# Expert feed-forward: who rounds the gated values, and in which order VectorE prepares the parts

## The reference, cut to what matters

```python
logits = x @ gate_w + gate_b
top_w, top_idx = jax.lax.top_k(softmax(logits), 2)      # 8 experts, 2 per token
h   = jax.nn.silu(x @ w1[e]) * (x @ w3[e])              # 256 -> 1024, for the chosen experts e
out = sum over the two experts of weight * (h @ w2[e])  # 1024 -> 256
x   = x + tanh(g_ffn[1]) * out
```

## Time and profile before

| | |
|---|---|
| median of 3 runs | 2627.19 us (2626.43 to 2630.02) |
| the profiled execution's own time | 2611.73 us |
| its span | 2610.0 us |
| TensorE matmul busy | 2107.1 us, 81% of the span |
| VectorE busy | 1935.4 us, 74% |
| ScalarE, GpSimd busy | 1022.2 us and 1016.1 us, 39% each |
| the 39 blocks | from about 1775 us to the end of the span |

### The profile page before, as it was taken

The page is one execution under the profiler, slowest core; times in us unless marked ns, Lnnn a source line. Parts: engine busy times, 40 slices in busy tenths (PEclk is TensorE's granted clock), DMA queues, the critical chain, the costliest instruction groups (busy, mean ns, idle before and its releaser), DMA issues. The chain is left out here.

```text
span 2610.0 us, 40439 instructions
## 1 busy us (share of the span) xinstructions
PE 2107.1 (81%) x13358; PEld 1479.3 (57%) x13358; DVE 1935.4 (74%) x3725; ACT 1022.2 (39%) x1581; POOL 1016.1 (39%) x554
## 2 busy tenths in 40 slices
PE   5898899747788888898888898406888888888887
PEld 3566666633234343434343435306888888888887
DVE  7999999837686867686768743605888888888886
ACT  2343344322355453545444453203444444444443
POOL 7988888622112030302021101273444444443343
PEclk9899999876799999999999998558999999999999
DMA  7000000021001010101010001233555555555552
GB/s 283 10 9 9 11 9 9 1 61 30 23 19 33 9 41 2 41 3 39 12 31 21 1 1 65 90 129 130 190 181 175 191 181 182 178 180 181 180 176 83
DMA packets 124788, 208.89 MB, mean 80 GB/s; under 512 B 9981, under 2 KB 88430, under 8 KB 124660
## 3 DMA queue, kind: packets, MB, share of 16 engines
q1 hardware_dynamic: 114024, 181.97, 20.9%
q0 software_dynamic: 10624, 25.26, 2.7%
q10 hardware_dynamic: 12, 0.01, 0.0%
HBM read 177.58 MB, written 33.18 MB: 81 GB/s over the span
## 5 line engine op out<-in xcount | busy, mean ns | idle before, releaser
L1218 DVE CUSTOM_DVE_ANT_0 x_dump<-x_ps,x_bias_q 128x512 bf16<-128x512 f32 x512 | 343.0, 690 | 66.5 <-PE x_ps L906 47.9
L1072 ACT ACTIVATE x_PT<-x_ps 128x1024 f32<-128x1024 f32 x256 | 255.0, 1021 | 311.0 <-PE x_ps L916 311.0
L843 POOL TENSOR_TENSOR x_rs<-x_ve,x_half 128x3 f32<-128x3 f32 x32 | 28.0, 876 | 719.6 <-DVE x_ve L1151 719.6
L1742 ACT ACTIVATE e_silu<-m_ps 128x256 f32<-128x256 f32 x312 | 118.8, 381 | 479.2 <-PE m_ps L1683 479.2
L906 PE MATMUL x_ps<-x_KS,x_QS 96*128 96x512 bf16 x512 | 207.5, 413 | 36.5 <-DVE x_mx L1218 33.4
L1781 DVE TENSOR_TENSOR e_gated<-e_silu,m_ps 128x256 f32<-128x256 f32 x312 | 122.4, 419 | 124.3 <-ACT e_silu L1742 115.3
L915 PE MATMUL x_ps<-x_bias_k,x_ident_b 128*128 128x512 bf16 x512 | 198.7, 388 | 19.2 <-issue 10.2
L1784 DVE CAST e_g_hi<-e_gated 128x512 fp32r<-128x512 f32 x156 | 209.4, 1343 | 5.3
L1683 PE MATMUL m_ps<-e_x_lo,m_hi 128*128 128x256 f32 x640 | 182.8, 286 | 26.0 <-issue 24.3
L1683 PE MATMUL m_ps<-e_x_lo,e_hi 128*128 128x256 f32 x608 | 180.3, 296 | 25.7 <-issue 25.7
L916 PE MATMUL x_ps<-x_QS,x_KS 99*128 99x512 bf16 x512 | 198.4, 388 | 0.0
(11 more groups left out here) (275 smaller groups left out, 6043.2 us busy)
## 6 DMA issues: line engine op xcount, KB each, us to landing
m_raw<-in_L_ffn_w_dram SPq DMA_DIRECT2D x117, 1024.0 KB, 5.2
expert_in<-a_blank SPq DMA_DIRECT2D x1, 10062.0 KB, 28.4
e_x<-expert_in SPq DMA_DIRECT2D x39, 258.0 KB, 8.1
x_mask_q<-in_mask_dram SPq DMA_DIRECT2D x32, 256.0 KB, 2.7
x_mask_k<-in_maskT_dram SPq DMA_DIRECT2D x32, 256.0 KB, 2.9
a_cT<-in_ctxT_dram SPq DMA_DIRECT2D x32, 128.0 KB, 2.2
x_cT<-in_ctxT_dram SPq DMA_DIRECT2D x32, 128.0 KB, 2.1
out_dram<-X SPq DMA_DIRECT2D x1, 4096.0 KB, 13.6
```

What stands on the lines that cost most here:

```text
L1072: act.activation(PT[u % 2][:, 2 * pr:2 * pr + 2, :], ps_st[pr], ACT.Exp).then_inc(exp_done[pr], 1)
L1218: dve.tensor_tensor_reduce(out=dump[i % 2][:, :], in0=bank, in1=bias_q[:, q, :], scale=1.0, scalar=NEG, op0=ALU.add, op1=ALU.max, accum_ou ...
L1742: act.activation(silu[f % 2][:, :], ps_h[f % 4][:, 0:BLK], ACT.Silu).then_inc(silu_done, 1)
```

## The change

The rounding `g_hi` leaves VectorE: ScalarE makes it, one pair at a time, in `gated_high`, after the silu of the following pair's first chunk. `gated` gets a second buffer, and VectorE makes the products of pair k before the difference of pair k - 1. The low part of the next block's matrix 1 moves from behind the gate into it, behind the difference of pair 1.

```diff
-            gated = sb("gated", [P, 2, BLK])
+            gated = two("gated", [P, 2, BLK])
...
+                def gated_high(j, k):
+                    act.wait_ge(gated_done, FC * j + 2 * k + 2)
+                    act.activation(g_hi[:, 2 * k:2 * k + 2, :], gated[k % 2][:, :, :], ACT.Copy).then_inc(g_high, 1)
...
                         act.activation(silu[f % 2][:, :], ps_h[f % 4][:, 0:BLK], ACT.Silu).then_inc(silu_done, 1)
+                        if f in (2, 4, 6):
+                            gated_high(j, f // 2 - 1)
                         if f in (1, 3, 5) and following:
                             high_part(act, j + 1, 1 - p, f // 2)
+                    gated_high(j, FC // 2 - 1)
...
-                    if not (isinstance(j, int) and j == 0):
-                        low_part(dve, j, p, 1)
...
+                    for k in range(FC // 2):
+                        if k > 1 or not (isinstance(j, int) and j == 0):
+                            dve.wait_ge(g_parts, FC // 2 * j + k - 1)
+                        for n in range(2):
+                            f = 2 * k + n
+                            dve.wait_ge(silu_done, FC * j + f + 1)
+                            dve.tensor_tensor(gated[k % 2][:, n, :], silu[n][:, :], ps_h[f % 4][:, BLK:2 * BLK], ALU.mult)\
                                 .then_inc(gated_done, 1)
-                        dve.wait_ge(gated_done, n + 1)
-                        steps.done(dve.tensor_copy(g_hi[:, f:f + 2, :], gated[:, :, :]))
-                        steps.wait()
-                        dve.tensor_tensor(g_lo[:, f:f + 2, :], gated[:, :, :], g_hi[:, f:f + 2, :].bitcast(F32), ALU.subtract)\
-                            .then_inc(g_parts, 1)
-                        if f == 0 and following:
-                            low_part(dve, j + 1, 1 - p, 0)
-                        dve.wait_ge(g_parts, FC // 2 * j + f // 2 + 1)
+                        if k:
+                            remainder(j, k - 1)
+                        if k in (0, 2) and following:
+                            low_part(dve, j + 1, 1 - p, k // 2)
+                    remainder(j, FC // 2 - 1)
+
+                def remainder(j, k):
+                    dve.wait_ge(g_high, FC // 2 * j + k + 1)
+                    dve.tensor_tensor(g_lo[:, 2 * k:2 * k + 2, :], gated[k % 2][:, :, :], g_hi[:, 2 * k:2 * k + 2, :].bitcast(F32), ALU.subtract)\
+                        .then_inc(g_parts, 1)
```

More of the change, by code:

```diff
@@ L1603, in experts @@
             silu_done, gated_done, g_parts = sem_("silu_done"), sem_("gated_done"), sem_("g_parts")
-            chain, y_left, y_out = sem_("chain"), sem_("y_left"), sem_("y_out")
+            g_high, y_left, y_out = sem_("g_high"), sem_("y_left"), sem_("y_out")
             labelled, blanks, before_in = sem_("labelled"), sem_("blanks"), sem_("before_in")
@@ L1759, in _ @@
             def _(dve):
-                steps = Steps(dve, chain)
                 def x_low(j, p):
@@ L1770, in x_low @@
                     dve.tensor_copy(label[p][:, :, :].bitcast(I32), xb[p][:, :, D:WIDE].bitcast(I32)).then_inc(labelled, 1)
-                    if not (isinstance(j, int) and j == 0):
-                        low_part(dve, j, p, 1)
                 def gate(j, i, p, following=True):
[L1776 to L1781, removed]
-                                .then_inc(gated_done, 1)
-                        dve.wait_ge(gated_done, n + 1)
-                        steps.done(dve.tensor_copy(g_hi[:, f:f + 2, :], gated[:, :, :]))
-                        steps.wait()
-                        dve.tensor_tensor(g_lo[:, f:f + 2, :], gated[:, :, :], g_hi[:, f:f + 2, :].bitcast(F32), ALU.subtract)\
-                            .then_inc(g_parts, 1)
-                        if f == 0 and following:
-                            low_part(dve, j + 1, 1 - p, 0)
-                        dve.wait_ge(g_parts, FC // 2 * j + f // 2 + 1)
+                    for k in range(FC // 2):
[5 more added lines that the diff above has]
+                            dve.tensor_tensor(gated[k % 2][:, n, :], silu[n][:, :], ps_h[f % 4][:, BLK:2 * BLK], ALU.mult)\
+                                .then_inc(gated_done, 1)
+                        if k:
[7 more added lines that the diff above has]
+                        .then_inc(g_parts, 1)
                 def add_y(j, p):
```

## The result

The changed kernel takes 2592.22 us (median of 4 runs, 2585.09 to 2597.55) against 2626.81 us of the kernel before beside it: ratio 0.9871, 95% interval 0.9836 to 0.9906. It is faster by 1.3%; 17 us slower had been forecast, and the time lies under the stated range. The profiled execution took 2588.63 us, its span is 2586.9 us. The expert blocks take 811 us of it (from TensorE's first transpose at 1775.87), before 835 us (from 1775.06): 24 us less in the profiled executions.

What follows compares the result with a forecast made beforehand. TensorE's two waits a block, 1.41 and 1.35 us, with VectorE and GpSimd excluding each other, were taken as the bound. Block -5, old falls -17, new falls +39 gave +17 us: 2628.7 profiled, 2644 by the median; range 2600 to 2675.

Steps and rivals of the forecast that it cites:

- The collision: Near the block's end, GpSimd's low part of matrix 2 locks out VectorE's difference of pair 2; TensorE waits 2.8 us.
- the "issue" wait: TensorE's wait at the block's end for VectorE's low part of matrix 1, 1.35 us a block, forecast to go.
- ScalarE's rounding: Rounding of 128x512 on ScalarE, taken as 0.60 us from the row of the same size, costing almost nothing.
- The landing of the scatter: Wait from scatter to gather on GpSimd, taken as about 2 us instead of 5.82 with loads spread out.
- The block: Next block starts at 2287.95 instead of 2288.09: -0.14 us, times 38 blocks -5 us.
- The clock: TensorE's clock falls from 2.4 to 1.2 GHz after the new 2.8 us wait in 26 of 38 blocks: +39 us.
- The falls of before: Eight stretches at TensorE's lower clock in the kernel before, taken to cost 17 us and to go.
- The price of 1.5 us a fall: Time a block loses when TensorE's clock falls after one idle piece, taken as 1.5 us.
- 8 in 13: Of 13 TensorE idle pieces of 1.74 us or more before, 8 were followed by a clock fall.
- The second rival: Same VectorE-GpSimd collision, but TensorE's clock holds as one lucky alignment repeats; 2605 to 2620 us, chance 0.16.
- the difference of 5.49 us: VectorE difference begun at 1854.47, 5.49 us instead of 0.69, cited as evidence that GpSimd's low part locks differences out.
- The rival of GpSimd getting in behind both differences: GpSimd enters after both last differences, TensorE becomes the bound; block some 17.8 us, 2494 us in all, chance 0.14.

Runs made afterwards that it cites:

- run with matrix 1 alone: Kernel before, with only the low part of the next matrix 1 moved inside the gate and the rounding left on VectorE; 2718.29 us, ratio 1.0384.
- the first experiment: Changed kernel, with GpSimd's low part of matrix 2 held back until the next labels are copied; 2478.63 us, ratio 0.9477.
- run with ScalarE's rounding alone: Changed kernel, with the low part of matrix 1 put back behind the gate, after the label copy; 2613.26 us, ratio 0.9989.

## Why the prediction was wrong, by its steps

- The collision: right. The place (difference of pair 2, behind the low part of matrix 1), the size of the wait (2.8 us worked out, 2.7 measured), its being one piece before the third pair, and the end of the "issue" wait came as written.
- ScalarE's rounding: 0.62 us against 0.60 taken. VectorE's low part of matrix 1 came 10.31 us into the block (2120.57, its first silu being at 2112.05, 1.79 us in), worked out as 10.35.
- The landing of the scatter: 2.23 us against 2 taken, before 5.82.
- The block: 20.47 us against 20.70. Two pairs of `project` behind the wait took 2.85 us, not 3.00, and GpSimd was done 0.09 us earlier. So -0.37 us a block, -14 us, where the sum had -5.
- The clock, the term that was mis-sized: the sum had 26 falls, +39 us. Measured are 2 from 1800 us on, some 3 us, and none in the last 36 blocks. The price of 1.5 us a fall was right, the number of falls was not.
- The falls of before: taken off at 17 us. In the trace of before the 22 blocks that meet no stretch at the lower clock are 20.83 us apart in the mean, like the reference block, and all 38 are 21.18, so they cost 13 us.
- Added up for the profiled executions: -14 for the block, -13 for the falls of before, +3 for the two left, -24 us, which is what the blocks lost. The medians lie 35 us apart, since the profiled execution of before was 15 us under its median and that of the changed kernel 4 us. No trace here shows where those other 11 us went.

The failed step is "I take a fall in 26 of 38 blocks, nearer to 8 in 13 than to all". It treated each wait as a draw of its own, at the rate of a kernel whose waits came at changing distances (its blocks last 20.4 to 22.6 us). In the changed kernel the same wait comes at one fixed distance, and what follows is regular: no fall in the last 36 blocks at 20.47 us; 35 falls with the block made 0.2 us longer; 21, four blocks in seven, with it made 0.4 us longer. The wait is 2.7 us in all three, and with most of it filled by transposes there is no fall. So the share forecast exists, but at another length of the block. Why 20.47 us is spared isn't shown. That the waits then keep one place against something periodic in the control of the clock fits the pattern of seven blocks, and is argued.

The second rival had the right case, with that reason ("one lucky alignment repeats"), at 0.16 and 2605 to 2620. With the shorter block its lower bound becomes 2596; 2592 was measured. No row of before could tell on which side the changed block would be, since 0.23 us, by which the forecast block of 20.70 was too long, is the step from 2 falls to 35. The chance of the second rival should have been higher; by how much, three lengths of the block can't say.

The Trainium skill (TensorE: Matmul & The Clock Gate, section "HAM oscillation — how this bites in real kernels") tells of a kernel in which a wait of some 3 to 5 us stands in every tile and every tile begins at the lower clock. The run with matrix 1 alone agrees: a wait of 3.7 us in each block, and a fall in all 38. At 2.7 us the runs go apart, with 2, 21 and 35 falls.

In one point the rows speak less clearly than the prediction says. It gives the difference of 5.49 us as agreeing with the rule it cites, that whoever issued first keeps the other out. But that difference is recorded from 1854.47 on, 0.37 us before GpSimd's low part at 1854.84. The exclusion agrees, the order in the profile does not; the last section has more on it.

The rival of GpSimd getting in behind both differences did not occur by itself; the first experiment shows its price: 17.53 us a block against 17.8 worked out, 2479 against 2494.

## What to carry to other kernels

Look first at which long instructions of VectorE and GpSimd can meet: two-input work in SBUF on both takes turns, and the one held back can be the short one on the path. Moving work between engines shifted that meeting for 35 us; telling GpSimd when to start gave 78 us alone and 140 us with the move. What a wait that recurs in every block costs in TensorE's clock can hang on the block's length: with the same wait of 2.7 us the clock fell 2 times, and 35 and 21 times in blocks made 0.2 and 0.4 us longer. So forecast it as cases, none and nearly all among them, not as a mean, and test it with a small pad.

## What the hardware showed that I had not expected

- The issue of an indirect DMA is held back by VectorE's two-input work as well: 2.30 us and 3.16 us instead of 1.03 in the rows above, each time beside a low part of 2.3 us on VectorE that had begun before it, and ending 0.9 us after that low part (2118.82 against 2117.90, 2106.82 against 2105.91).
- The start that the profile gives doesn't always tell who goes first. In the trace of before eight differences are recorded as begun 0.15 to 0.53 us ahead of GpSimd's low part. In seven GpSimd had stood idle for 0.27 us or more, and VectorE went first. In the eighth, the one of 5.49 us, GpSimd came straight from its gather, 0.03 us after it, and VectorE was kept out:

```profile
1853.80 1.01 POOL L1640 DMA_INDIRECT e_y<-out_dram,e_label  x1 [0.31 <-issue]
```

  In the run with ScalarE's rounding alone 13 more differences are like the eighth: recorded 0.08 to 0.66 us ahead of GpSimd's low part, which stands 0.02 to 0.03 us behind its gather, and lasting 5.2 to 5.8 us. So in all 14 GpSimd won when it came straight from a gather. Why isn't shown.
- Some 0.2 us more of a block of 20.5 us changed the falls of the clock from 2 to 35, and the time by 56 us.
